# A buffer of its own for the magnitude of the feed-forward branch, and the semaphore that lets GpSimd overwrite its staging tile

## What is computed

```
xn  = layernorm(x)                                  # x: (8, 4096, 1024)
q, k, v = xn @ Wq, xn @ Wk, xn @ Wv                 # 8 heads of 64, segments of 256 rows
# per segment: memory read (elu(q)+1) @ mem / ((elu(q)+1) @ z), then mem, z += this segment
# att = gate * memory read + (1 - gate) * softmax(q k^T / 8) v
real = xn @ cos(theta + theta_noise)                # 1024 x 1024
imag = xn @ sin(phi + phi_noise)
out  = x + att @ Wo + sqrt(real*real + imag*imag)
```

## Time and profile before

| what | value |
|---|---|
| median of 3 runs (lowest to highest) | 1720.52 us (1720.38 to 1722.41) |
| the profiled execution's own time | 1720.74 us |
| span of its slowest core, core 7 | 1719.0 us |
| spans of the 8 cores | 1713.5 to 1719.0 us |
| mean granted TensorE clock of the cores, share of 2.4 GHz | 0.764 to 0.771 |
| busy on core 7: PE, DVE, ACT, POOL | 760.5, 691.0, 336.4, 216.6 us |

### The profile page before, as it was taken

How to read it: one execution, slowest core, us unless ns; L and a number is a source line. 1 busy time by engine, 2 the same in 40 slices (tenths; PEclk the granted TensorE clock), 3 DMA queues, 4 the chain that set the end, 5 groups by cost and what they waited for, 6 DMA issues and landing times.

```text
span 1719.0 us, 14707 instructions; the slowest of 8 cores (1713.5 to 1719.0 us)
## 1 busy us (share of the span) xinstructions
PE 760.5 (44%) x5125; PEld 415.4 (24%) x5125; DVE 691.0 (40%) x1409; ACT 336.4 (20%) x828; POOL 216.6 (13%) x127
## 2 busy tenths in 40 slices
PE   0000436455454626364454536264554536263653
PEld 0000214132222313132322223141322222131321
DVE  0000445354443544354444435453544435443540
ACT  0110211122130302121121303111221313021212
POOL 1111001100111111101011111111001111111013
PEclk9999858777685858677786858687776868686787
DMA  9555000000101010000001010100001010100001
GB/s 172 112 128 126 1 25 2 25 26 1 51 1 50 2 49 2 29 22 17 35 0 49 3 49 2 49 2 25 27 1 50 1 50 2 49 2 0 27 1 49
DMA packets 18121, 56.49 MB, mean 33 GB/s; under 512 B 1217, under 2 KB 5249, under 8 KB 18050
## 3 DMA queue, kind: packets, MB, share of 16 engines
q0 software_dynamic: 8000, 20.97, 6.0%
q1 hardware_dynamic: 10050, 34.59, 5.7%
HBM read 41.98 MB, written 16.78 MB: 34 GB/s over the span
## 4 chain that ended last, share of the span: by engine, by line
PE 35%; DVE 26%; ACT 13%; DMA 8%; issue 7%; POOL 4%; DVEq 4%; POOLq 2%; ACTq 1%
PE pb L120 9%; ACT e_bf L291 7%; PE pb L456 6%; PE pb L340 5%; DVE pT_sb L594 5%; DVE negm L567 4%; PE pb L351 3%; PE pb L363 3%; DMA stage<-th 3%; DVE xnT_sb L519 2%; POOL stage L244 2%; DVE attT_bf L630 2%; DMA stage<-thn 2%; DMA stage<-phn 2%; DVEq L503 2%
## 5 line engine op out<-in xcount | busy, mean ns | idle before, releaser
L237 POOL TENSOR_TENSOR stage<-fscr 128x1024 f32<-128x1024 bf16 x32 | 61.2, 1913 | 1284.3 <-ACT fscr L135 699.3
L329 PE MATMUL pb<-ident_sb,xn_bf 128*128 128x128 bf16 x256 | 29.8, 309 | 433.6 <-DVE xn_bf L511 433.6
L120 PE MATMUL pb<-sin_r,xnT_sb 128*128 128x512 bf16 x512 | 163.2, 490 | 116.3 <-ACT fscr L135 116.3
L291 ACT ACTIVATE e_bf<-pb,negms 128x256 bf16<-128x256 f32 x256 | 117.2, 484 | 196.5 <-DVE negms L572 196.5
L456 PE MATMUL pb<-wo_r,attT_bf 128*128 128x512 bf16 x256 | 109.2, 604 | 71.1 <-DVE attT_bf L630 71.1
L120 PE MATMUL pb<-cos_r,xnT_sb 128*128 128x512 bf16 x512 | 134.5, 423 | 0.0
L594 DVE CAST pT_sb<-pb 128x512 bf16<-128x512 f32 x128 | 79.5, 683 | 131.3 <-PE pb L398 131.3
L329 PEld LDWEIGHTS pb<-ident_sb,xn_bf 128*128 128x128 bf16 x256 | 26.0, 143 | 434.5 <-issue 434.5
L143 ACT ACTIVATE stage<-stage,cbias 128x1024 f32<-128x1024 f32 x32 | 36.7, 1148 | 456.5 <-POOL stage L244 455.1
L120 PEld LDWEIGHTS pb<-sin_r,xnT_sb 128*128 128x128 bf16 x512 | 59.5, 120 | 220.0 <-issue 193.9
L152 DVE TENSOR_TENSOR out_sb<-out_sb,stage 128x1024 f32<-128x1024 f32 x32 | 39.1, 1222 | 164.1 <-ACT stage L146 164.1
(11 more groups left out here) (85 smaller groups left out, 1058.6 us busy)
## 6 DMA issues: line engine op xcount, KB each, us to landing
x_sb<-x SPq DMA_DIRECT2D x16, 1024.0 KB, 4.8
y<-out_sb SPq DMA_DIRECT2D x16, 1024.0 KB, 4.0
stage<-th POOLq DMA_DIRECT2D x4, 1024.0 KB, 5.2
stage<-thn POOLq DMA_DIRECT2D x4, 1024.0 KB, 9.0
stage<-ph POOLq DMA_DIRECT2D x4, 1024.0 KB, 5.1
stage<-phn POOLq DMA_DIRECT2D x4, 1024.0 KB, 8.5
wq_b<-wq POOLq DMA_DIRECT2D x1, 1024.0 KB, 16.9
wk_b<-wk POOLq DMA_DIRECT2D x1, 1024.0 KB, 23.0
```

What stands on the lines that cost most here:

```text
L120: li = t_.matmul(pb[6 + half][:, :], xnT_sb[:, ppf + 256 * dt + 128 * u: ppf + 256 * dt + 128 * u + 128], w_s[:, 1024 * dt + 512 * half: 1 ...
L237: g.tensor_mul(stage[:, 0:1024], fscr[:, 0:1024], fscr[:, 0:1024])
L291: sc.activation(e1_bf[:, 2048 * u + 256 * h: 2048 * u + 256 * h + 256], sl, AF.Exp, bias=negms[:, c:c + 1], scale=0.125, accum_out=den[:, ...
L329: li = t_.matmul(pb[2 + dt // 2][:, 128 * (2 * (dt % 2) + u): 128 * (2 * (dt % 2) + u) + 128], xn_bf[:, 1024 * u + 128 * dt: 1024 * u + 12 ...
```

## The change

A new tile `magb` (128 x 2048, bfloat16) is added, with one half for each `u`. L146 writes the magnitude there and no longer into `stage`, and L152 reads it from there. POOL's wait ahead of L237 is for `s_mag` (L146 of the round before has read `stage`) where it was for `s_r2` (L152 of the round before). Since `magb` is used again one chunk later, `ffn_mag` gets a wait of its own, from the second feed-forward chunk on, for the L152 that read the same half one chunk earlier. Nothing else is changed: the instructions and their order on each engine are the same.

```diff
+    magb = sbt("magb", [128, 2048], BF16)
...
         def ffn_mag(sc, tf, u):
+            if tf >= 1:
+                sc.wait_ge(s_r2, 2 * (tf - 1) + u + 1)
             sc.wait_ge(s_ss, 2 * tf + u + 1)
             sc.drain()
             sc.activation(stage[:, 1024:2048], stage[:, 0:1024], AF.Ln,
                           bias=cbias[:, 2:3])
             sc.drain()
-            sc.activation(stage[:, 0:1024], stage[:, 1024:2048], AF.Exp,
+            sc.activation(magb[:, 1024 * u:1024 * u + 1024],
+                          stage[:, 1024:2048], AF.Exp,
                           scale=0.5).then_inc(s_mag, 1)
...
                          out_sb[:, ppf + 1024 * u:ppf + 1024 * u + 1024],
-                         stage[:, 0:1024]).then_inc(s_r2, 1)
+                         magb[:, 1024 * u:1024 * u + 1024]).then_inc(s_r2, 1)
...
                     if 2 * t + u >= 1:
-                        g.wait_ge(s_r2, 2 * t + u)
+                        g.wait_ge(s_mag, 2 * t + u)
                     g.wait_ge(s_sqf, 8 * t + 4 * u + 2)
```

## The result

The changed kernel takes 1573.36 us (median of 9 runs) against 1720.89 us for the kernel before on the same chips (10 runs). The ratio is 0.9141, with a 95% interval of 0.9131 to 0.9150; one run of each kernel, in which the cores of a die had a lower granted clock (1605.25 and 1768.67 us), is left out of the ratio. The forecast was 1569.6 us, range 1560 to 1591. The profiled execution took 1573.61 us, and its slowest core, core 3, spans 1572.0 us; its profile is read here.

What follows compares the result with a forecast made beforehand. Bound by a chain hopping between engines, with POOL, DVE and ACT waiting in a ring; boundaries 128.8 + run-out 11.1 + clock 14 - POOL's hold 3 = 150.9 us off 1720.74: 1569.8, as median 1569.6 us; range 1560 to 1591.

Steps and rivals of the forecast that it cites:

- The ring: At chunk ends POOL waits for DVE, ACT for POOL, DVE for ACT; opening this gains 14 x 9.20 = 128.8 us.
- a slack of 12.8 us for 12.9: Both magnitudes lie ready before DVE's first L152 at the chunk's end, with 12.9 us to spare.
- ACT's new wait: ACT's wait on s_r2 ahead of L143, for the previous boundary's L152, costs nothing: the cover is a whole chunk.
- the type: Writing and reading the magnitude in bfloat16 instead of float32: bounded by -0.1 and +0.2 us each per chunk, taken as 0.
- The clock: PE's bursts meet the granted clock elsewhere: -1.0 us a period, bounds -1.4 to +0.5, 14 us gained over 14 periods.
- the forecast 140.0: Forecast gain in us over the 14 periods behind a boundary, with 2.8 of POOL's 3 us cost counted there.
- POOL's new place: POOL's half 1 instructions run beside DVE's L608 to L630 and hold L608: 0.2 us a chunk, 3 us taken.
- The run-out: After the last chunk: no sin matmul wait (7.8 us), no slow stretch (2.0), earlier last L237 (1.3); together 11.1 us.
- The last square's 1.3 us: In the run-out the last L237 goes with L146, one L152 and a hand-over sooner, gaining 1.3 us.

Runs made afterwards that it cites:

- the run with the buffer only: The changed kernel with magb and ACT's new wait kept, but POOL's wait put back on s_r2 (DVE's add): 1723.21 us, ratio 0.9999 to the kernel before.
- The worst place: The changed kernel with POOL's half 1 round also waiting for s_am, so its square starts about 0.3 us ahead of DVE's L612: 1616.19 us, ratio 0.9368.
- the run in which only the end was opened: The changed kernel with POOL waiting on s_r2 again, except on s_mag for the last two chunks' feed-forward rounds: 1712.53 us, ratio 0.9948.
- early statistics: The changed kernel with next chunk's statistics in DVE's wait for the output projection, normalization before the feed-forward adds, run-out add delayed: 1478.64 us, ratio 0.8599.

## Why the prediction was right

**The ring.** Right in place and size: 9.21 us for 9.20 at the boundary, a slack of 12.8 us for 12.9, and the buffer alone brings nothing.

**ACT's new wait and the type.** Next to nothing, as forecast. The run in float32 shows it for the type. ACT's new wait never ended its idle time; only the very last logarithm starts 0.41 us behind POOL's sum instead of 0.13, in this kernel and in the run with the buffer only. What these 0.28 us are was not tried.

**The clock.** The sign and nearly the size were right: forecast -1.0 us a period, with a choice between -1.4 and +0.5 that was argued, not known. The chunk of the earlier trace rows and the changed kernel's chunk from 1032.53 on show the difference. PE rows of the kernel before, and then of the changed kernel:

```profile
1027.00 5.01 PE L340 MATMUL pb<-xnT_sb,wq_b 128*128 128x256 bf16 x32 [2.81 <-DVE xnT_sb L519]
...
1043.65 1.05 PE L386 MATMUL pb<-kT_bf,qT_bf 64*128 64x256 bf16 x8 [4.24 <-DVE sk_bf L549]
...
1052.39 5.30 PE L120 MATMUL pb<-sin_r,xnT_sb 128*128 128x512 bf16 x16 [3.03 <-ACT fscr L135]
```

```profile
1035.16 5.89 PE L344 MATMUL pb<-xnT_sb,wq_b 128*128 128x256 bf16 x32 [2.80 <-DVE xnT_sb L523]
...
1052.69 0.62 PE L390 MATMUL pb<-kT_bf,qT_bf 64*128 64x256 bf16 x8 [4.24 <-DVE sk_bf L553]
...
1061.01 3.61 PE L121 MATMUL pb<-sin_r,xnT_sb 128*128 128x512 bf16 x16 [2.45 <-ACT fscr L136]
```

The q projection lost 0.88 us; the scores gained 0.43, the first sin block 1.69. The two output projections went from 3.57 and 3.25 us to 3.37 and 3.57, +0.12 together. That is -1.12 us. With 9.21 from the ring and 0.07 lost at L612 it makes 10.26, against 10.24 between the settled periods. That it came out near -1.0 is in part luck. The argument for it was that a disturbed rhythm shows short periods first, and on the slowest core the first ones were the long ones (85.67, 85.57 and 87.03 us before 85.33). The worst place shows that the clock's part can as well go against a change. Over all 14 periods the ring gave 128.9 us and the meeting with POOL took 1.0, so the clock's part of the 139.5 us is 11.6, where 14 were forecast. That the whole still came within 0.5 us of the forecast 140.0 is because POOL's new place cost 1.8 us less than was taken.

**POOL's new place.** The mechanism is shown and the size was too high: 0.07 us a chunk for the forecast 0.2, 1 us for 3. The estimate had L237 end at 1080.1 behind a start of L608 at 1079.87. In the run L241 ends 0.21 us behind L612's start (1085.13 + 1.89 to 1086.81), and L612 is longer by only 0.07. The traces show why: the late one of the two is longer by the overlap less 0.14 us, each time. L612 overlaps by 0.21 us and is 0.07 longer. L245 starts 0.41 us ahead of L612's end and is 0.27 longer (2.16 us for 1.89). In the worst place L614 overlaps by 1.60 us and is 1.46 longer, and in the run-out L241 by 1.13 us and 0.99. The estimate priced the overlap in full. The page "SBUF — State Buffer" of the Trainium skill, section "SBUF: two separate sides", holds up in both directions: POOL held DVE (2.15 us for 0.69), and DVE held POOL (2.88 for 1.89). Its exclusive lock for the whole instruction would cost the late one the whole overlap; measured it is 0.14 us less.

**The run-out.** This term was mis-sized: 8.4 us for 10.9. The last square's 1.3 us were counted without asking whom POOL would now meet; it starts together with DVE's add, which takes 1.0 of them back, and ACT's late last logarithm takes 0.3. From the start of the exponential before it to the start of the last add it was 11.50 us in the kernel before (1701.89 to 1713.39) and is 11.44 now. The rest is clock: the step kept the cos block at 3.63 us, and in the changed kernel it took 5.60 us, with some 0.7 us made up elsewhere. The run in which only the end was opened has both: the cos block takes 5.54 and 5.58 us on cores 5 and 7, whose ends take 112.4 and 112.6 us, and on the six other cores, with ends of 111.1 to 111.3 us, it takes 3.63 (on two of them 3.40 us are recorded for 15 of the 16 matmuls).

**The start.** 0.9 us went into the load of the weights and the first period, where nothing was changed. The run with the buffer only, whose time is that of the kernel before, has its first L523 at 182.05, so this much is scatter.

## What to carry to other kernels

When three engines wait for one another in a ring, ask which of the waits protects data and which only an old choice of where a result is put. A small buffer for the result lets the producer go on with the reader far behind, and the time is in the wait that it makes unnecessary, not in the buffer. Work that fills a gap on one engine has to be finished off the chain on all the others, or it is no filler. Behind it, look at what has become the pause: here the statistics and the deviation were the next 6.9 us, and DVE had an idle place for them.

## What was not expected of the hardware

The period settles to the same value within 0.2 us for many chunks: 95.57 us before, 85.33 after, 78.50 with early statistics. With one more instruction of 0.60 us it doesn't settle. With a hold of 1.46 us it takes 88.91 in one stretch and 85.35 in another, while each of its two sin blocks takes 5.30 or 3.61 us. So a change in this kernel, whose PE is granted 1.2 and 2.4 GHz by turns, isn't worth its length alone: 18 us added cost 27.5, 22 us cost 34 to 44.

A POOL instruction that starts first holds a DVE instruction with two SBUF inputs to its end (2155 ns at most for 693 at the median). A DVE instruction of that kind that starts 0.1 us earlier than POOL's holds POOL in turn (2.88 us for 1.89). The late one is longer by the overlap less 0.14 us, so a short meeting is cheaper than it looks. Reading PSUM, with or without one input in SBUF, DVE was not held (0.42 and 0.15 us beside POOL and without it).
